# Top-k attention of a decoder: the selection written as a difference of exponentials, and three queues in another order

## The reference, cut to what matters

```python
Q = (x_text @ Wq).reshape(Bb, Tt, H, DH)
K = (x_vision @ Wk).reshape(Bb, Gg, H, DH)
scores = jnp.einsum('bthd,bghd->bhtg', Q, K) / np.sqrt(DH).astype(np.float32)
scores = jnp.where(vision_mask[:, None, None, :], scores, -jnp.inf)
topv, topi = jax.lax.top_k(scores, K_TOP)          # K_TOP = 32
probs = jax.nn.softmax(topv, axis=-1)
attn = jnp.zeros_like(scores).at[bi, hi, ti, topi].set(probs)
attn_mean = attn.mean(axis=1)
V = x_vision @ Wv
c_t = jnp.einsum('btg,bgd->btd', attn_mean, V)
c_t = c_t * text_mask[..., None]
```

## Time and profile before

| | us |
|---|---|
| median of three runs (2393.81, 2394.77, 2398.04) | 2394.77 |
| the profiled execution's own time | 2396.02 |
| its span, first to last instruction | 2394.2 |
| VectorE's selection, first MAX8 to last MATCH_REPLACE8 | 1733.4 to 2047.7 |

### The profile page before, as it was taken

The page is one execution under the profiler, slowest core; times in us unless marked ns, Lnnn a source line. Parts: engine busy times, 40 slices in busy tenths (PEclk is TensorE's granted clock), DMA queues, the critical chain, the costliest instruction groups (busy, mean ns, idle before and its releaser), DMA issues.

```text
span 2394.2 us, 37754 instructions
## 1 busy us (share of the span) xinstructions
PE 2103.9 (88%) x15300; PEld 1469.6 (61%) x15300; DVE 1514.4 (63%) x3047; ACT 711.3 (30%) x1407; POOL 810.4 (34%) x726
## 2 busy tenths in 40 slices
PE   6988979999999978999999999988567767879986
PEld 2334337777766656888888888776445555446632
DVE  7998955566333325556556555666398998737556
ACT  6445324333311222232223222222142222121132
POOL 3242448966500014444444444432270000013101
PEclk9768689999899989999999999999766675889998
DMA  5222173222010027101001000100231110310001
GB/s 154 70 75 90 57 161 92 60 67 71 7 53 1 1 94 173 34 1 69 1 2 51 19 1 1 52 1 1 71 100 29 30 30 25 87 49 1 0 0 31
DMA packets 67181, 114.47 MB, mean 48 GB/s; under 512 B 34153, under 2 KB 58722, under 8 KB 65794
## 3 DMA queue, kind: packets, MB, share of 16 engines
q1 hardware_dynamic: 67010, 112.07, 16.3%
HBM read 91.56 MB, written 33.34 MB: 52 GB/s over the span
## 4 chain that ended last, share of the span: by engine, by line
PE 64%; DVE 25%; POOL 6%; issue 3%; ACT 2%; DMA 0%; SPq 0%; DVEq 0%; POOLq 0%; ACTq 0%
PE PS L1534 8%; PE PS L1550 8%; PE PS L1280 5%; PE PS L1258 4%; DVE top L2334 4%; DVE w_s L2343 4%; PE PS L2214 2%; DVE ln_st L270 2%; PE PS L2204 2%; PE PS L1447 2%; PE PS L1461 2%; PE PS L2143 2%; PE PS L892 2%; PE PS L879 2%; PE PS L409 2%
## 5 line engine op out<-in xcount | busy, mean ns | idle before, releaser
L289 POOL TENSOR_SCALAR ln_ve<-ln_mv 128x2 f32<-128x2 f32 (+1 forms) x87 | 20.0, 230 | 1195.5 <-DVE ln_mv L273 1195.4
L1807 POOL TENSOR_TENSOR q_x<-q_f,cols 128x2048 f32<-128x2048 f32 x56 | 217.9, 3911 | 9.7 <-ACT q_f L1638 8.0
L1762 DVE TENSOR_TENSOR p_x<-PS,cols 128x1024 f32<-128x1024 f32 x112 | 129.3, 1218 | 134.3 <-PE PS L1496 134.3
L1089 DVE TENSOR_REDUCE XD<-PS 112x2 f32<-112x750 f32 x128 | 120.0, 940 | 96.0 <-PE PS L879 95.6
L457 PE MATMUL PS<-bc_parts,ident 96*128 96x448 bf16 x256 | 106.0, 518 | 41.2 <-DVE st_h L691 28.0
L1048 ACT ACTIVATE e_t<-PS 125x672 f32<-125x672 f32 x128 | 93.5, 730 | 154.8 <-PE PS L892 154.8
L1337 DVE SCALAR_TENSOR_TENSOR XA<-PS,gate_w,XA 112x256 f32<-112x256 f32 x128 | 56.0, 480 | 125.6 <-PE PS L1280 125.6
L2096 PE MATMUL PS<-dg,e_p 112*125 112x112 f32 x384 | 80.1, 400 | 61.7 <-ACT dg L2292 61.7
L1625 ACT ACTIVATE wb<-PS,cols 128x256 f32<-128x256 f32 x224 | 90.8, 472 | 142.8 <-PE PS L1534 142.8
L879 PE MATMUL PS<-enc_w,q_s 32*112 32x375 f32 x512 | 130.6, 535 | 1.7 <-DVE XD L1089 1.7
L892 PE MATMUL PS<-q_s,enc_w 32*125 32x112 f32 x1536 | 121.9, 289 | 2.6 <-ACT e_t L1048 2.6
(11 more groups left out here) (366 smaller groups left out, 4710.6 us busy)
## 6 DMA issues: line engine op xcount, KB each, us to landing
k_full_scratch<-k_scratch SPq DMA_DIRECT2D x112, 112.0 KB, 2.9
v_all_scratch<-v_st SPq DMA_DIRECT2D x16, 750.0 KB
v_t<-v_all_scratch SPq DMA_DIRECT2D x16, 750.0 KB
t_ring<-k_full_scratch SPq DMA_DIRECT2D x8, 784.0 KB, 12.4
enc_w<-in_enc_w SPq DMA_DIRECT2D x2, 3072.0 KB, 11.2
wc<-in_enc_w SPq DMA_DIRECT2D x2, 3072.0 KB, 12.2
k_all_scratch<-k_st SPq DMA_DIRECT2D x16, 375.0 KB
enc_w<-k_all_scratch SPq DMA_DIRECT2D x64, 93.8 KB, 3.5
```

The lines of the kernel that those rows point to most:

```text
L1089: dve.tensor_reduce(nm_w[0:T, g % 4, 64 * half + 16:64 * half + 49:32], PS[0:T, 2 * half:2 * half + 2, 0:S2], AX.X, ALU.max, negate=True). ...
L1762: last = dve.tensor_tensor(p_x[:, m, :, :, :], ps[1][:, m * P:(m + 1) * P].rearrange("p (h i) -> p h i", i=16).unsqueeze(2) .to_broadcast( ...
L1807: last = pool.tensor_tensor(q_x[:, c, :, :].rearrange("p t (h i) -> p t h i", i=16), q_f[:, k % 2, c, :].rearrange("p (t i) -> p t i", i=1 ...
```

## The change

The instruction L2353 goes from VectorE's queue. In its place ScalarE writes exp(`w_s` - largest) over `w_s`, which is zero where `w_s` is FILL and equals `e_p` elsewhere, and exp over the 32 values that `top8` now keeps for each head, with their sum (`rest_and_sum`); GpSimd subtracts `w_s` from `e_p`, which leaves the 32 chosen, and divides as a power of -1. `w_s` and `top8` have four slots in place of two. Two waits are new on VectorE: the first MAX8 of a head waits for `x_rest` of the same head a row before, and its first MATCH_REPLACE8 for `x_cut` of it. GpSimd's normalizations are spread over the rows, one behind each subtraction. The mask and the ones beside it are bfloat16. TensorE makes keys two rows ahead in place of one, the scores of heads 0 and 1 with them, and those of heads 2 and 3 behind `gather`. ScalarE's order follows. `s4x_load` is as it was.

```diff
-        w_s = sb("w_s", [T, 2, S2], pool=s4a)
-        mskb = sb("mskb", [P, S2], pool=s4a)
+        w_s = sb("w_s", [T, XH, S2], pool=s4a)
+        mskb = sb("mskb", [P, S2], BF16, pool=s4a)
...
-                if 1 <= b < B - 1:
-                    uses.append(("k", b + 1))
+                if b + 2 < B:
+                    uses.append(("k", b + 2))
                 uses += [("at", b), ("m1", b)]
...
-                    pe.matmul(ps[h][0:T, 0:S2], ident[r, 32 * h + b:32 * h + b + 1].to_broadcast([32, T]), mskb[r, :],
+                    pe.matmul(ps[h][0:T, 0:S2], ident16[r, b:b + 1].to_broadcast([32, T]), mskb[r, :],
                               start=False, stop=True).then_inc(x_s_ready, 1)
...
-            for j in range(B // 2):
+            scores(1, (0, 1))
+            for j in range(B // 4):
                 turn_rows(j)
-            for b in range(B):
-                if b + 1 < B:
-                    if b >= 1:
-                        topk_keys(pe, b + 1)
-                    scores(b + 1)
-                    attend(b)
-                    gather(b)
-                    if b % QB == QB - 1:
-                        values(b // QB)
+            scores(1, (2, 3))
+            for j in range(B // 4, B // 2):
+                turn_rows(j)
+            for b in range(B - 1):
+                if b + 2 < B:
+                    topk_keys(pe, b + 2)
+                    scores(b + 2, (0, 1))
+                attend(b)
+                gather(b)
+                if b + 2 < B:
+                    scores(b + 2, (2, 3))
+                if b % QB == QB - 1:
+                    values(b // QB)
...
+            def rest_and_sum(b, h):
+                act.wait_ge(x_sel, XH * b + h + 1)
+                bias = neg_m[:, h:h + 1]
+                act.activation(w_s[:, h, :], w_s[:, h, :], ACT.Exp, bias=bias)
+                tops = top8[:, h, :, :].rearrange("t r v -> t (r v)")
+                act.activation(tops, tops, ACT.Exp, bias=bias, accum_out=e_sum[:, b % 2, h:h + 1])\
+                    .then_inc(x_rest, 1)
+
+            def weights(b):
+                act.wait_ge(x_rs, b + 1)
+                for h in range(XH):
+                    last = act.activation(dg[:, b % 2, h, :], ident[0:T, 0:T], ACT.Copy,
+                                          scale=e_rs[:, b % 2, h:h + 1])
+                last.then_inc(x_dg, 1)
...
-                    if b >= 1 and h == 1:
-                        copy_attention(b - 1)
-                        copy_context(b - 1)
-                        if b + 1 < B:
-                            copy_keys(b + 1)
-                act.wait_ge(x_rs, b + 1)
-                for h in range(XH):
-                    last = act.activation(dg[:, b % 2, h, :], ident[0:T, 0:T], ACT.Copy,
-                                          scale=e_rs[:, b % 2, h:h + 1])
-                last.then_inc(x_dg, 1)
+                    if h == 1:
+                        if b == 0:
+                            copy_keys(1)
+                        else:
+                            if b == 1:
+                                for j in range(B // 4, B // 2):
+                                    copy_rows(j)
+                            if b + 1 < B:
+                                copy_keys(b + 1)
+                            weights(b - 1)
+                        rest_and_sum(b, 0)
+                        rest_and_sum(b, 1)
+                    elif h == 3:
+                        if b == 0:
+                            for j in range(B // 4):
+                                copy_rows(j)
+                        else:
+                            copy_attention(b - 1)
+                        rest_and_sum(b, 2)
+                        rest_and_sum(b, 3)
+                        if b >= 1:
+                            copy_context(b - 1)
+                            if b % QB == 0:
+                                copy_values(b // QB - 1)
...
                             if turn == 0:
                                 dve.wait_ge(x_s_ready, n + 1)
+                                if b >= 1:
+                                    dve.wait_ge(x_rest, n - 3)
...
+                            if turn == 0 and b >= 1:
+                                dve.wait_ge(x_cut, n - 3)
...
-                        dve.wait_ge(x_exp, n + 1)
-                        e = e_p[:, XH * (b % 2) + h, :]
-                        last = link.mark(dve.scalar_tensor_tensor(e, w_s[:, a, :], FILL, e, ALU.is_equal, ALU.mult,
-                                                                  accum_out=e_sum[:, b % 2, h:h + 1]))
-                    link.after(last)
-                link(dve.reciprocal(e_rs[:, b % 2, :], e_sum[:, b % 2, :]))
-                dve.tensor_scalar(e_rs[:, b % 2, :], e_rs[:, b % 2, :], tmk[:, b:b + 1], 1.0 / XH,
-                                  ALU.mult, ALU.mult).then_inc(x_rs, 1)
...
             for b in range(B):
...
+                for h in range(XH):
+                    n = XH * b + h
+                    pool.wait_ge(x_rest, n + 1)
+                    e = e_p[:, XH * (b % 2) + h, :]
+                    pool.tensor_tensor(e, e, w_s[:, h, :], ALU.subtract).then_inc(x_cut, 1)
+                    if h == XH - 1:
+                        link(pool.tensor_tensor(e_rs[:, b % 2, :], e_sum[:, b % 2, :], minus[:, :], ALU.pow))
+                        pool.tensor_scalar(e_rs[:, b % 2, :], e_rs[:, b % 2, :], tmk[:, b:b + 1], None,
+                                           ALU.mult).then_inc(x_rs, 1)
```

More of the change, by code:

```diff
@@ L155, in build @@
         dg = sb("dg", [T, 2, XH, T], pool=s4a)
-        at_t = sb("at_t", [JR, 2, JC, T], pool=s4a)
+        minus = sb("minus", [T, XH], pool=s4a)
+        at_t = wa[0:JR, :, :].rearrange("p k n -> p (k n)")[:, 0:2 * JC * T].rearrange("p (z j t) -> p z j t", z=2, j=JC)
         msk8 = sb("msk8", [P, S2], U8, pool=s4a)
@@ L662, in ssm_dve @@
             dve.wait_ge(const_loaded, 80)
-            for k in range(3):
+            for k in range(4):
                 last = dve.tensor_copy(ident16[32 * k:32 * k + 32, 0:32], ident[32 * k:32 * k + 32,
@@ L2057, in topk_masks @@
             pool.tensor_scalar(mskb[:, :], msk8[:, :], -1.0, -FAR, ALU.add, ALU.mult).then_inc(e_prep, 1)
-            pool.tensor_scalar(tmk[:, :], tmk8[:, :], 1.0, None, ALU.mult).then_inc(e_prep, 1)
+            pool.tensor_scalar(tmk[:, :], tmk8[:, :], 1.0 / XH, None, ALU.mult).then_inc(e_prep, 1)
+            link(pool.memset(minus[:, :], -1.0))
         def s4x_pe(pe):
@@ L2076, in turn_rows, with scores @@
                 last.then_inc(m_ready, 1)
-            def scores(b):
+            def scores(b, heads):
                 pe.wait_ge(m_used, max(m_count("k", b), m_count("q", b // QB)) + 1)
-                for h in range(XH):
+                for h in heads:
                     n = XH * b + h
@@ L2122, in s4x_pe @@
             pe.wait_ge(e_prep, 3)
-            scores(0)
+            scores(0, range(XH))
             queries(2)
@@ L2258, in copy_context, with copy_values @@
                 act.copy(m1[0:CR[1], 1, b * T:(b + 1) * T], bank[0:CR[1], T:2 * T]).then_inc(m_used, 1)
[L2259 to L2263, removed]
+            def copy_values(q):
+                for c in range(KC):
+                    act.copy(c_t[:, c, q * QT:(q + 1) * QT], m_bank(act, "ct", 2 * q + c)[:, 0:QT])\
+                        .then_inc(m_used, 1)
+            def rest_and_sum(b, h):
[11 more added lines that the diff above has]
+                last.then_inc(x_dg, 1)
             def copy_rows(j):
@@ L2275, in s4x_act @@
                     n = XH * b + h
[L2276 to L2279, removed]
                     act.wait_ge(x_first, n + 1)
@@ L2332, in s4x_dve @@
                                 link.after(cut[a])
-                            s = ps[h][0:T, 0:S2] if turn == 0 else w_s[:, a, :]
-                            found[a] = link.mark(dve.max(top8[:, a, turn, :], s))
+                            s = ps[h][0:T, 0:S2] if turn == 0 else w_s[:, h, :]
+                            found[a] = link.mark(dve.max(top8[:, h, turn, :], s))
                         if turn == 0:
@@ new lines, in norm_scale, with norm_shift @@
+            def norm_scale(g):
+                x = xn_rows[g]
+                n = sum(a == g for a, i in XN_AT)
+                link(pool.tensor_tensor(x, x, e_row4("g_in")[:, 0:n, :], ALU.mult))
+            def norm_shift(g):
+                x = xn_rows[g]
+                n = sum(a == g for a, i in XN_AT)
+                pool.tensor_tensor(x, x, e_row4("b_in")[:, 0:n, :], ALU.add).then_inc(x2_affine, 1)
+            for b in range(B):
+                for h in range(XH):
[7 more added lines that the diff above has]
+                                           ALU.mult).then_inc(x_rs, 1)
+                    if XH * 2 <= n < XH * 2 + B:
+                        norm_row(n - XH * 2)
+                    elif XH * 2 + B <= n < XH * 2 + B + 10:
```

(5 more changed lines are left out.)

57 lines of the change are left out of this document (28 added, 29 removed).

## The result

The changed kernel takes 2406.32 us (median of 19 runs, 2395.48 to 2411.52) against 2395.35 us before (19 runs, 2392.05 to 2399.92). The ratio is 1.0041, 95% interval 1.0030 to 1.0051: slower by 11 us. The forecast was 2379 us, with a range of 2343 to 2401 and a chance of 0.12 for slower. The profiled execution took 2408.12 us, its span is 2406.0.

The account below looks back on a forecast made before the run. VectorE bounds the selection now; afterwards mostly TensorE's chain at mixed clock. Selection 293.5 for 314.3, -20.8, end +2.4 + 3, together -15.4: 2396.0 becomes 2380.6, the median 1.3 lower, so 2379 us, range 2343 to 2401.

Parts of the forecast that it names:

- With 68% of the time at half clock as now: TensorE in the selection: today's half-clock share was kept, giving a turn of 14.4 + 0.68 x 5.9 = 18.4 us.
- The chain: Each selection turn: load, keys, copy, diagonals or scores, attend, copy, gather, load; 14.4 us at full clock, 20.3 at half.
- the second rival: Selection: TensorE's idle wait keeps half clock, 13 turns take 20.3 us, +16.7 in all, 2411 us; chance of slower 0.12.
- point of decision: Selection: the slower case decides from 19.4 us a row, a half clock's share of 85%.
- L2353 goes with its two losses: VectorE in the selection: 39.7 us of work and 18.9 of losses go; alone it finishes in 254.7, 59.6 earlier.
- GpSimd does not slow VectorE: Selection: MATCH_REPLACE8 keeps its mean of 542 ns while GpSimd works beside it.
- ScalarE and GpSimd covered: Selection: their added work fits their idle time, ScalarE 150 us and GpSimd 126 us of 255.
- The chain's terms at half clock: Selection turn: 5.9 + 3.11 + 0.55 + 1.9 + 5.37 + 0.55 + 2.92 = 20.3 us.
- The chain at full clock, 14.4: Selection turn: 14.4 us at full clock, which hides under VectorE's row of 15.92.
- VectorE's idle time, 30 to 45 us: Selection: VectorE idles at first MAX8 or MATCH_REPLACE8 for scores, `x_rest` or `x_cut`, 30 to 45 us in all.
- The end of the stage, +2.4 and +3: After the last match: diagonals done after 5.0 us, not 2.6, +2.4; last rows' products perhaps at half clock, +3.
- at even odds: Stage's end: last rows' attend, gather and values may find half clock, 7.3 us more, taken as +3.

Follow-up runs that it names:

- two forms: New selection with TensorE's order of the kernel before: 2414.26 us; the same with ScalarE's exponentials of the rests moved ahead of its copies: 2418.32 us.
- additional products: Changed kernel plus 12 or 24 products with the identity, into unread columns, ahead of the keys of rows 3 to 15: 2392.22 or 2374.34 us.
- the selection alone: Changed kernel's selection with the order of TensorE and ScalarE as before, keys one row ahead, loads as before: 2414.26 us.
- early loads: Changed kernel with SyncE's load of ctx_f for row b+1 put ahead of its wait for gather(b-2): 2346.25 us.

## Why the prediction was wrong

All times beside the kernel before (2395):

| selection | order | loads | us |
|---|---|---|---|
| old | old | as before / early | 2395 / 2394.8 |
| old | new | as before / early | 2406.5 / 2379.9 |
| new | old | as before, two forms | 2414.3, 2418.3 |
| new | new | as before / early | 2406.3 / 2346.3 |

**The step that failed** is the one clause "With 68% of the time at half clock as now". The share was taken from the trace of before and carried over to another order of TensorE's work and waits. Measured: (1 - 0.53) / 0.5 = 94%. The chain itself was found in its place and with its parts, and the second rival is what happened, with its own sign: a granted clock near 0.5 and rows over 20 us. It gave 2411 us, its point of decision was a share of 85%, and the time is 2406. Its selection was 321.3 us, measured 324.6; its span would have grown by 16.7, measured 11.8.

The text weighed exactly this. Rows of before spoke both ways, 5.37 us for an `attend` that TensorE had waited for the earlier trace rows against a mean of 0.66. I let the mean decide, though it described a stage with another pattern of waits, and gave the other case 0.12.

The Trainium skill, page "TensorE: Matmul & The Clock Gate", section "Part 1: The HAM clock gate", says that waits for a DMA inside a loop throw the clock back each time around. By that rule the time was the rival's, and this trace agrees: 0.50 through 149 and 154 us, broken only for 7. The runs with additional products make it more than an agreement, since there only TensorE's activity differs and the clock rises to 0.68 and 0.83.

One thing the prediction overlooked: it took TensorE's wait in each turn for something new. TensorE of the kernel before waited once a turn too, for the diagonals (1733 to 2060: total us, times, longest):

```profile
PE PS L2096 <- ACT dg L2292: 61.7, 13, 7.7
```

Its clock came back to full in many of these turns, as in that of the earlier trace rows, where the gather took 1.61 us. With the selection alone TensorE waited for diagonals even longer, up to 11.3 us at a time, and the clock was 0.69. So a wait in each turn does not by itself say which level the chain will have. That filling this wait brings the clock back is shown; why a wait for the diagonals lets it come back and the wait for the load did not stays open.

Point by point:

- *L2353 goes with its two losses, VectorE alone 254.7 us.* Right. With the load out of the way rows take 15.96 us and the selection 259.0, of which 3.4 are a wait for GpSimd.
- *GpSimd does not slow VectorE.* Right. MATCH_REPLACE8 is 533 ns with 125 us of GpSimd's work beside it, 542 before, where L2353 had suffered. The Trainium skill, page "SBUF — State Buffer", section "Who interferes with whom", says that a VectorE instruction with two SBUF inputs contends with GpSimd's reads and that one with at most one, outside the modes that use both ports, does not. L2353 is of the first kind. MAX8 and MATCH_REPLACE8 are of the second (the eight values to be replaced come by an instruction of their own, MATCH_VALUE_LOAD in the timeline), and the rows agree.
- *ScalarE and GpSimd covered.* Right, in this order of queues. The pair of exponentials with its read of the sum is 601 ns and some 0.2 more when it follows closely (0.80 from 1908.87 to 1909.67 in the trace of after), not 0.98; the subtraction 0.982, not 0.95; the power 1.039 for 1.06. VectorE waited 14.5 + 3.0 = 17.5 us for the two engines in all, 5.5 of them at once before 1800 and never more than 2.4 at a time behind it; with the early loads 3.4 us are left of it.
- *The chain's terms at half clock.* Load from the end of the gather to the keys 1948.58 - 1941.95 = 6.6 us, not 5.9. Keys and their copy 3.72 (3.66). Two heads' scores with the mask 1933.09 - 1931.25 = 1.84 (1.9). `attend` and its copy 5.96 (5.92), gather 2.90 (2.92). In all 21.0 for this turn. Thirteen rows take (2058.06 - 1783.58) / 13 = 21.1, with values in three of them, for which VectorE's row is 23.35 (three times), against 20.3 + 3.2 = 23.5.
- *The chain at full clock, 14.4.* Right: 14.8 with the products that fill the wait.
- *VectorE's idle time, 30 to 45 us.* It was 56.6 + 17.5 = 74 us, as the rows are those of the second rival.
- *The end of the stage, +2.4 and +3.* The diagonals are done 5.3 us after the last match (5.0 forecast). The last `attend` ran at full clock, 2.84, though the clock had been at half until 2056. From the last match to the span's end 347.9 us against 346.5: +1.4. In the run with early loads the same stretch is 355.1 us, with the last `attend` at 5.35 us. What I had put at even odds came out one way here and the other way there.

The sum with the measured terms: selection +10.4, end +1.4, together +11.8, the difference of the two spans.

## What to carry to other kernels

When a product moves forward in a queue, follow its loads back to what releases them: here a DMA stood behind a wait on another queue that used to be met a turn earlier, and it closed a chain round three engines. Where TensorE waits inside such a chain, price the chain at both clock levels, and do not settle between them by the mean clock of the stage as it was: a mean clock belongs to the pattern of work in which it was measured. Here the chain was longer than VectorE's row at half clock and shorter at full, and that decided between a loss and a gain. And when a change is slower, look at what the freed engine waits for before undoing it: one edit of SyncE's loads made this one 2.1% faster than before.

## What was unexpected of the hardware

Additional products on the engine whose chain bounded the stage made the kernel faster: 24 products, together 5.6 to 10.5 us, in each of 13 turns, and 32 us less in all. The gain comes through the clock, 0.53 to 0.81 in the selection.

The busy share does not rank the clocks. In the changed kernel TensorE was busy for 251 of 324.5 us and granted 0.53; before for 228 of 314.3 and granted 0.66; with the selection alone for 214 of 346.5 and granted 0.69. Much of that is that the same work takes longer at half clock. Busy time multiplied by the granted clock, as an estimate of the work, gives shares of 0.41, 0.48 and 0.43. With 12 additional products it gives 0.60 at a clock of 0.68, so the clock does not follow this share either. What sets when the clock returns in a pattern like these was not settled.
